# Attention layer on eight cores: the order of the column-split probability-times-value matmuls

## The reference

```python
x = _layernorm(x + attn(x, Wq, Wk, Wv, Wo))      # x: (4, 4096, 1024)
x = _layernorm(x + ffn(x, W1, b1, W2, b2))

# attn, per head of size 64
scores = einsum('bqhd,bkhd->bhqk', q, k) * SCALE
scores = SOFTCAP * tanh(scores / SOFTCAP)
mask   = (j <= i) & (j > i - WINDOW)
p = softmax(where(mask, scores, NEG), axis=-1)
o = einsum('bhqk,bkhd->bqhd', p, v)
return o @ Wo.T

# ffn
_quantize(W) = clip(round(W / (mean(abs(W)) + EPS)), -1, 1)
h = relu(x @ _quantize(W1).T + b1);  return h @ _quantize(W2).T + b2
```

## Time and profile before

| | us |
|---|---|
| median of 4 runs (1770.34 to 1827.27) | 1771.57 |
| profiled execution, its own time | 1770.93 |
| its span on the slowest core, core 6 | 1769.2 |
| spans of the 8 cores | 1727.8 to 1769.2 |

### The profile page before, as it was taken

The page is one execution under the profiler, slowest core; times in us unless marked ns, Lnnn a source line. Parts: engine busy times, 40 slices in busy tenths (PEclk is TensorE's granted clock), DMA queues, the critical chain, the costliest instruction groups (busy, mean ns, idle before and its releaser), DMA issues. The chain is left out here.

```text
span 1769.2 us, 23954 instructions; the slowest of 8 cores (1727.8 to 1769.2 us)
## 1 busy us (share of the span) xinstructions
PE 1131.4 (64%) x8095; PEld 608.3 (34%) x8196; DVE 581.8 (33%) x751; ACT 744.9 (42%) x668; POOL 226.6 (13%) x277
## 2 busy tenths in 40 slices
PE   5795467676666666666650199516777899366770
PEld 2352244444444444444430044202222344122220
DVE  0346434555555555565553500211000100212101
ACT  2231688988787878787500043101000234011000
POOL 1000000000101010110121000360000000621304
PEclk9897567778787878788765599857777899699775
DMA  9999532223233433354346222302221123132301
GB/s 146 216 254 284 148 96 90 84 77 104 80 118 91 108 91 107 102 104 95 78 132 180 94 77 78 137 0 91 76 71 66 36 78 131 72 143 95 119 24 48
DMA packets 127062, 186.69 MB, mean 106 GB/s; under 512 B 11104, under 2 KB 93024, under 8 KB 122848
## 3 DMA queue, kind: packets, MB, share of 16 engines
q1 hardware_dynamic: 103632, 131.14, 25.8%
q0 software_dynamic: 23312, 54.01, 11.8%
HBM read 161.53 MB, written 35.65 MB: 111 GB/s over the span
## 5 line engine op out<-in xcount | busy, mean ns | idle before, releaser
L532 PE MATMUL spsP<-QT,KTd 64*128 64x128 bf16 x2304 | 138.0, 241 | 258.3 <-ACT Tst L550 189.9
L550 ACT ACTIVATE Tst<-spsP 128x1024 f32<-128x1024 f32 x256 | 262.2, 1024 | 90.3 <-PE spsP L541 56.6
L1087 PE MATMUL f2ps<-hT,w2b 128*128 128x512 bf16 x1004 | 281.7, 446 | 6.6 <-DMA w2b<-w2q_t 3.4
L1041 PE MATMUL f1ps<-x2bf,w1b 128*128 128x512 bf16 x1003 | 225.3, 385 | 88.3 <-PEq L84 87.0
L569 ACT ACTIVATE Pst<-Tst,cm 128x4608 bf16<-128x4608 f32 x64 | 264.7, 4136 | 13.5 <-ACT Tst L556 13.3
L625 DVE RECIPROCAL den_sb<-pvd 128x256 f32<-128x256 f32 x64 | 112.5, 1758 | 259.8 <-PE pvd L609 259.8
L1114 ACT CAST t_bf<-x 128x512 bf16<-128x512 f32 x32 | 19.8, 617 | 406.9 <-DVE x L1107 406.9
L532 PEld LDWEIGHTS spsP<-QT,KTd 64*128 64x128 bf16 x2304 | 78.9, 101 | 288.1 <-issue 288.0
L1087 PEld LDWEIGHTS f2ps<-hT,w2b 128*128 128x128 bf16 x1024 | 115.3, 113 | 175.9 <-issue 95.4
L1041 PEld LDWEIGHTS f1ps<-x2bf,w1b 128*128 128x128 bf16 x1024 | 101.4, 99 | 212.4 <-issue 95.0
L1054 ACT ACTIVATE hT<-f1ps,b_sb 128x512 bf16<-128x512 f32 x128 | 88.0, 687 | 136.2 <-PE f1ps L1041 130.0
(11 more groups left out here) (80 smaller groups left out, 933.2 us busy)
## 6 DMA issues: line engine op xcount, KB each, us to landing
qin<-w1T SPq DMA_DIRECT2D x64, 512.0 KB, 5.9
qin<-w2T SPq DMA_DIRECT2D x64, 512.0 KB, 6.0
w2b<-w2q_t SPq DMA_DIRECT2D x32, 1024.0 KB, 4.8
w1b<-w1q_t SPq DMA_DIRECT2D x64, 256.0 KB, 2.7
w1q_t<-qout POOLq DMA_DIRECT2D x32, 256.0 KB, 4.3
r1d<-r1f POOLq DMA_DIRECT2D x64, 128.0 KB, 5.3
w2q_t<-qout POOLq DMA_DIRECT2D x32, 256.0 KB, 5.0
outT<-x POOLq DMA_DIRECT2D x4, 2048.0 KB, 7.7
```

What stands on the lines that cost most here:

```text
L532: sp=last_in_bank: e.matmul(ps[:, col:col + 128], lhsT, rhs, start=st, stop=sp),
L550: lambda e, ps=ps, kbp=kbp: e.activation(Tst[:, kbp * 1024:(kbp + 1) * 1024], ps[:, 0:1024], AF.Tanh, scale=1.0 / 240.0),
L1041: lambda e, dc=dc, nt=nt, wslot=wslot, pslot=pslot: e.matmul(f1ps[pslot][:, :], w1b[wslot][:, dc * 128:(dc + 1) * 128], x2bf[:, dc * 1024 ...
L1087: lambda e, fc=fc, nt=nt, wslot=wslot, pslot=pslot: e.matmul(f2ps[pslot][:, :], w2b[wslot][:, fc * 128:(fc + 1) * 128], hT[:, fc * 1024 + ...
```

## The change

The two loops of `emit_pv` are turned inside out. Before, for each key block `rel` the matmul of parity 0 is followed by that of parity 1. After, all nine key blocks of parity 0 are issued, then all nine of parity 1; the same holds for the denominators. The instructions, their operands, their count (36 per group, with 36 weight loads), the first waits and the last signal are the same.

```diff
@@ -576,10 +576,10 @@
                     qt, kv = divmod(g, 4)
                     P = Pst[g % 2]
                     pd = pvd
-                    for rel in range(NREL):
-                        ca = qt + rel
-                        vt = Vv[:, ca * 256 + kv * 64: ca * 256 + kv * 64 + 64]
-                        for par in range(2):
+                    for par in range(2):
+                        for rel in range(NREL):
+                            ca = qt + rel
+                            vt = Vv[:, ca * 256 + kv * 64: ca * 256 + kv * 64 + 64]
                             w0 = []
                             if par == 0 and rel == 0:
                                 w0.append(("A", exp_done[g]))
```

## The result

The changed kernel takes 1791.62 us (median of 7 runs, 1786.05 to 1831.23) against 1770.96 us (median of 10). The ratio is 1.0124, 95% interval 1.01 to 1.0147: 22 us slower. Ratios here are of undisturbed executions only; the longest times, such as 1831.23, come from executions in which one half of the cores ran at a lower clock. The forecast was 1806.1, 35 us slower, in a range of 1784 to 1876. Direction and place came as forecast, and the time lies in the range, near its lower end; the working behind the 35 us is not what happened, as the rows show.

What follows compares the result with a forecast made beforehand. In attention ACT mostly sets the pace, at times waiting for PE's first piece. Ordinary groups +15.4, statistics waits +7.3, groups 3 to 16 +8.4, ends +1.5 and +2.0 make +34.6 us: 1806.1 us, range 1784 to 1876.

Steps and rivals of the forecast that it cites:

- Pairs overlap, one half alone doesn't gain: L593 and L609: both parities run at once, a pair costing what one would; neighbours on the same half follow one another.
- 33 steps: L593 and L609: the 36 matmuls, 18 steps before, become 33 because two overlap only at the three parity crossings.
- Loads hidden: L593 and L609: weight loads cost nothing more; the rival "exposed loads" gave about +162 us, 1934 us, chance 0.04.
- One group in three starts low: Ordinary groups 17 to 62: one in three starts L593 at the low clock, 2.1 us late; 0.75 us a group.
- The 15 of 16 high starts behind late ends: Kernel before: of 16 late ends 15 were followed by a high start, which speaks for high starts after the change.
- The rise 3.6 us after the start: Groups starting low: clock rises 3.6 us after L593 starts, so 17 steps low and 16 high, 5.5 us (+1.5).
- The sum: Whole kernel: 15.4 + 7.3 + 8.4 + 1.5 + 2.0 = 34.6 us slower.
- The ordinary groups: 41 groups within 17 to 62: ACT waits longer for PE's first piece, 30.9 less the present 15.5, +15.4 us.
- the five waits: PE's waits for the statistics steps (L759): ACT's wait grows by all that L609 ends later, 38.7 less 31.4, +7.3 us.
- groups 3 to 16: Attention groups without projection unit: two in three start low and are 0.9 us late, +8.4 us.
- the ends: Attention stage: +1.5 us at group 3, behind DVE's threshold reductions, and +2.0 in the last two groups.
- All of it passed on: The whole 34.6 us reaches the total, since projection tail, barrier and feed-forward start when attention ends and are untouched.

Runs made afterwards that it cites:

- either loop alone: Parities apart in only the V loop (L593) or only the denominator loop (L609), against the kernel before: 1.0118 and 1.0127.
- the parity-0-first one: All 18 matmuls of parity 0 (V, then denominators), then all 18 of parity 1, against the kernel before: 1.0579, +103 us.
- runs of five: Both loops issue five key blocks of parity 0, the same five of parity 1, then four and four, against the kernel before: 0.9978.
- runs of three: Both loops issue three key blocks of parity 0, then the same three of parity 1, and so on, against the kernel before: 1.0013.
- the spread projection: Late statistics matmul, projection unit's eight matmuls moved into the tanh stretch, against the kernel before: 0.9774 with the old order, 0.9898 with the changed order.

## Why the prediction was right, and where not

1. **Pairs overlap, one half alone doesn't gain: right.** Single matmuls of one half take 213 ns each at 1.2 GHz, like a pair, and 110 ns at 2.4 GHz.
2. **"Where the stream crosses from one parity to the other (three times in 36) can two still overlap", 33 steps: wrong.** It is 24. A matmul starts ahead of up to three that wait before it. Shown by the starts in the changed kernel, in either loop alone (23 steps), the parity-0-first one (32) and runs of five (19), by runs of three costing nothing, and by either loop costing as much as both. With 24 steps a high group takes 24 x 0.112 + 0.07 = 2.76 us, +0.7 and not +1.68; the one shown with the spread projection took 2.83.
3. **Loads hidden: right**, by the 213 and 110 ns.
4. **One group in three starts low: wrong.** Of the 46 starts in groups 17 to 62, 40 are low, against 22 before. The 15 of 16 high starts behind late ends didn't carry over. Nor did the six high starts stay high, which the forecast took for granted: the clock fell 0.1 to 0.7 us after the start and stayed low for 3.4 us, the 36 matmuls took 4.4 us, and ACT waited 0.87 to 0.89 us, longer than behind most low starts. One of them, windows before and after the fall, and ACT's wait:

```profile
376.77:377.43 0.66, 0.66 (x8) 0.66 (x9) 0.42 (x1) 0.51 (x2) 0.19 (x1) 1.00 0.00 0
377.43:380.84 3.41, 3.41 (x30) 2.93 (x29) 0.83 (x2) 3.21 (x2) 0.90 (x2) 0.50 0.47 155
```
```profile
383.22 4.54 ACT L550 ACTIVATE Tst<-spsP 128x1024 f32<-128x1024 f32 x4 [0.89 <-PE spsP L541]
```

So the clock at the start is the wrong thing to count; the time that a run of matmuls spends low is what ACT feels.

5. **The rise 3.6 us after the start: not what happened in either stretch.** It was the mean of groups 4 to 12 before. In the 40 low starts of groups 17 to 62 it comes 2.4 us after, in the mean (4.2 in the 22 before), and in groups 5 to 16 of the changed kernel 4.5 to 4.7 us after, nearly at the end of the run. In the group shown, 2.21 us low are 10.4 steps, the other 13.6 go at 112 ns, in all 2.21 + 1.52 + 0.07 = 3.80 us (3.84 in the rows), where the forecast for a low start was 5.5. With 1.85 + 0.17 behind them and 5.39 allowed, 0.47 us late; measured, 0.61 less the usual 0.15. So a low group takes no longer than a low one did before (3.98 us), in spite of its six more steps; the loss is that nearly every group is now one.
6. **The sum: in its range partly by luck.** It came out 13 us high because a step count too large outweighed a share of low starts too small. With 24 steps and the rest of the prediction's working as it stands, a high group is on time and a low one 3.6 + 0.8 + 0.07 + 1.85 + 0.17 - 5.39 = 1.1 us late. The ordinary groups then give 41 x 1.1/3 - 15.5 = -0.5 us, the five waits about +2, groups 3 to 16 nothing, the ends about 1: some 3 us in all, an estimate, where 22 were measured. With that one error put right and the others left, the forecast would have missed. Before, ACT waited 0.7 to 1.1 us in about every second ordinary group; after, it waits 0.3 to 0.9 us in nearly all, 0.15 of it the usual. PE's 36 matmuls start over 2.87 us before and 3.78 after (means of groups 17 to 62), 0.9 us more a group, while the period grew by only 15.3/46 = 0.33. The rest fell into the slack of the groups that had been on time.
7. **All of it passed on: right.** Tail and feed-forward changed by 0.8 and -2.0 us.

Open: why nearly all groups start low after the change, and take turns in the version with the spread projection. The rows show that it is so, and the runs don't tell what sets it. Also open is whether the look-ahead counts matmuls or matmuls with their weight loads. Each has a load of its own here, and nothing that takes one away was tried.

## What to carry to other kernels

When two streams use different column halves of the array, interleave them, but they needn't alternate one by one: runs of three and of five cost nothing measurable here (18 and 19 steps), and runs of nine cost a third more steps (24). Count steps of a split stream by the look-ahead, over the whole stream and not loop by loop. And before pricing a longer run on one engine, find which instruction another engine waits for behind it; moving a unit of work and a waiting matmul out of that path was worth 40 us here, nearly twice what the order of the matmuls was. A forecast that hits can rest on errors that cancel: compare its terms, not only its sum.

## What the hardware showed that was not expected

Matmuls started out of program order: L609 at 530.97, ahead of L593 at 531.11, 531.22 and 531.33, on the other column half, with three before them waiting. The Trainium skill ("TensorE: Matmul & The Clock Gate", "Part 3: Packing small matmuls — row/col tiling") calls matmuls strictly in order in start and end. The starts here contradict that for different column tiles; within one half the order held in the groups that I read one by one.

One line of the same section lets a weight load overlap running matmuls only when the row group differs (its paragraph on the mechanism also allows a load into a background weight buffer). Nine matmuls on one half and all 128 rows, each with its own load, took 1.92 us at 1.2 GHz, which is the bare 256 columns each and leaves no time for a load; here too the measurement decides.
